# Moving the first norming of x and its transposes for the next chunk from half-steps 1 to 8 to half-steps 43 to 55 of the chunk in front

## The reference

```python
x = x + _L0_attn_ref(_layernorm(x, axis=-1), ...)   # q, k, v, rope, softmax(q k^T / 4) v, Wo
x = x + _L0_ffn_ref(_layernorm(x, axis=-1), ...)    # rms norm, top 2 of 8 experts, gated GELU-like unit
```

## Time and profile before

| | us |
|---|---|
| median of 3 runs | 1080.0 |
| lowest, highest | 1079.83, 1082.15 |
| profiled execution | 1079.36 |
| its span, first to last instruction | 1077.6 |
| PE busy | 945.4 |
| DVE busy | 759.1 |
| ACT busy | 749.9 |
| POOL busy | 402.8 |

### The profile page before, as it was taken

How to read it: one execution, slowest core, us unless ns; L and a number is a source line. 1 busy time by engine, 2 the same in 40 slices (tenths; PEclk the granted TensorE clock), 3 DMA queues, 4 the chain that set the end, 5 groups by cost and what they waited for, 6 DMA issues and landing times. The chain is left out here.

```text
span 1077.6 us, 16615 instructions
## 1 busy us (share of the span) xinstructions
PE 945.4 (88%) x5288; PEld 398.2 (37%) x5288; DVE 759.1 (70%) x1514; ACT 749.9 (70%) x1018; POOL 402.8 (37%) x341
## 2 busy tenths in 40 slices
PE   4669998899888997989899998889998999998396
PEld 2312213244332443334343443424442444344264
DVE  5851112689658885688858887588977786789797
ACT  1458895868668785877758786687878887885252
POOL 3515205343355324543353533653342333233310
PEclk9869999999899998999999998999999999999799
DMA  5273463424535452444533245354454453423021
GB/s 168 91 164 94 95 138 86 108 70 107 122 75 140 108 115 73 114 106 107 129 84 107 87 110 114 74 139 96 112 124 100 109 127 85 104 61 103 27 67 35
DMA packets 79984, 109.76 MB, mean 102 GB/s; under 512 B 22530, under 2 KB 56722, under 8 KB 76818
## 3 DMA queue, kind: packets, MB, share of 16 engines
q1 hardware_dynamic: 61460, 83.47, 33.2%
q10 hardware_dynamic: 18432, 25.17, 8.1%
HBM read 82.90 MB, written 25.69 MB: 101 GB/s over the span
## 5 line engine op out<-in xcount | busy, mean ns | idle before, releaser
L890 ACT ACTIVATE probs<-S 128x1024 f32<-128x1024 f32 x512 | 512.8, 1024 | 156.0 <-PE S L739 154.1
L739 PE MATMUL S<-Qs,Ks 98*128 98x512 bf16 x1024 | 301.4, 387 | 20.2 <-ACT probs L890 16.6
L753 PE MATMUL OP<-probs,V 128*17 128x512 f32 x2048 | 275.0, 609 | 3.6 <-ACT O L899 3.6
L977 POOL TENSOR_TENSOR act_lo<-act_sb,act_hi 128x512 fp32r<-128x512 f32 x112 | 150.2, 1344 | 112.9 <-ACT act_hi L879 112.8
L725 PE MATMUL D<-W,act_hi 128*128 128x256 f32 x448 | 132.9, 328 | 25.8 <-issue 14.4
L1196 DVE SCALAR_TENSOR_TENSOR acc<-D,combh,acc 128x256 f32<-128x256 f32 x224 | 97.6, 477 | 81.7 <-PE D L725 81.3
L739 PEld LDWEIGHTS S<-Qs,Ks 98*128 98x128 bf16 x1024 | 78.9, 99 | 204.0 <-ACT probs L890 97.8
L971 POOL TENSOR_SCALAR W<-W2b 128x512 fp32r<-128x512 bf16 x64 | 41.5, 650 | 238.3 <-PE D L725 193.2
L1204 DVE SCALAR_TENSOR_TENSOR th_sb<-th_sb,g_sb 128x512 f32<-128x512 f32 x112 | 109.2, 975 | 16.4 <-ACT th_sb L866 12.8
L725 PE MATMUL D<-W,act_lo 128*128 128x256 f32 x448 | 114.1, 286 | 0.0
L725 PEld LDWEIGHTS D<-W,act_hi 128*128 128x128 f32 x448 | 86.7, 194 | 51.2 <-issue 20.6
(11 more groups left out here) (173 smaller groups left out, 1007.2 us busy)
## 6 DMA issues: line engine op xcount, KB each, us to landing
W<-in_w ACTq DMA_DIRECT2D x64, 256.0 KB, 2.8
Ks<-k_scr SPq DMA_DIRECT2D x32, 384.0 KB
W2b<-in_w ACTq DMA_DIRECT2D x64, 128.0 KB, 2.8
Ks<-k_scr SPq DMA_DIRECT2D x32, 256.0 KB
o_scr<-O SPq DMA_DIRECT2D x32, 256.0 KB, 4.3
Qs<-q_scr SPq DMA_DIRECT2D x32, 192.0 KB
k_scr<-parts SPq DMA_DIRECT2D x12, 384.0 KB, 3.3
q_scr<-parts SPq DMA_DIRECT2D x12, 384.0 KB, 3.4
```

The lines of the kernel that those rows point to most:

```text
L739: last = mm(S[:, j2, C * i:C * (i + 1)], Ks[0:SROWS + MROWS, g % 2, j, P * kt:P * (kt + 1)], Qs[0:SROWS + MROWS, g % 2, j, :], start=True, ...
L753: last = mm(OP[32 * j:32 * j + VW, :], V[:, kt, HG * g + j, :], probs[:, s % 2, C * j:C * (j + 1)], start=kt == 0, stop=kt == KT - 1)
L890: nc.scalar.activation(probs[:, s % 2, 2 * C * j2:2 * C * (j2 + 1)], S[:, j2, :], ACT.Exp, scale=SCALE).then_inc(exp_done, 1)
L977: tt(act_lo[:, e % 2, it, :], act_sb[:, a % 2, :], act_hi[:, e % 2, it, :].bitcast(FP32), ALU.subtract).then_inc(lo_s, 1)
```

## The change

The four stages of the first norm and the two transposes leave PREP and form a table of their own, AHEAD. AHEAD in window u prepares chunk u + 3 (the one after the chunk whose queries and keys PREP makes in the same window), at half-steps 43 (`stats1`), 45 (`rstd1`), 49 (`xn`), 50 (`x_next`), 54 and 55 (`xT0`, `xT1`). In the next window the query/key tiles and values read `xnT` at the half-steps at which they read it before. Window 0 does both: the old places for chunk 2 (table PREP_FIRST) and AHEAD for chunk 3. So AHEAD runs in windows 0 to 4, and windows 1 to 5 have nothing of the norm in half-steps 1 to 8. In a half-step AHEAD comes after PREP and before POST and EXPERTS. The number of instructions of each kind in the kernel stays the same. The counters of the fillings are now counted in one pass, instead of restarted from computed constants, with the same meaning.

```diff
 
 
-    AT = {"x_next": 8, "stats1": 1, "rstd1": 1, "xn": 4, "xT0": 7, "xT1": 8, "qk0": 10, "qk1": 12, "qk2": 22,
+    AT = {"stats1": 43, "rstd1": 45, "xn": 49, "x_next": 50, "xT0": 54, "xT1": 55, "qk0": 10, "qk1": 12, "qk2": 22,
           "qk3": 30, "rope": 2, "part1": 3, "length": 5, "part2": 7, "part3": 10, "v0": 37, "v1": 42, "gmax": 1,
           "guard": 4, "flag": 6, "x1_in": 0, "wo_0": 8, "x1_b": 11, "wo0": 13, "wo1": 14, "stats2": 15, "rstd2": 16, "xc": 17, "ss":
           18, "ms": 18, "rrms": 20, "nf": 22, "nfT": 24, "logits": 26, "gates1": 26, "etop": 27, "gates2": 28,
           "combT": 32, "b20": 33, "b21": 34}
     FFN0, LAG, PAIRED = 26, 4, True
     DOWN, TANH, HIDDEN, UP, HI, LO, W2AT = 0, 2, 2, 1, 4, 6, 3
-    PREP = {}
+    PREP, PREP_FIRST, AHEAD = {}, {}, {}
     POST = {}
     EXPERTS = {}
 
     def place(table, half, *stages):
         table.setdefault(divmod(half, 2), []).extend(stages)
 
-    for st in ("x_next", "stats1", "rstd1", "xn"):
-        place(PREP, AT[st], (st, 0))
-    for a in range(2):
-        place(PREP, AT[f"xT{a}"], ("xT", a))
-        place(PREP, AT[f"v{a}"], ("v", a))
-    for a in range(4):
-        h = AT[f"qk{a}"]
-        place(PREP, h, ("qk", a))
-        for st in ("rope", "part1", "length", "part2", "part3"):
-            place(PREP, h + AT[st], (st, a))
-    for st in ("gmax", "guard", "flag"):
-        place(PREP, h + AT["length"] + AT[st], (st, 0))
-
+    FIRST = {"stats1": 1, "rstd1": 1, "xn": 4, "x_next": 8, "xT0": 7, "xT1": 8, "qk0": 10, "qk1": 12}
+    for table, at in ((AHEAD, AT), (PREP_FIRST, FIRST)):
+        for st in ("x_next", "stats1", "rstd1", "xn"):
+            place(table, at[st], (st, 0))
+        for a in range(2):
+            place(table, at[f"xT{a}"], ("xT", a))
+    for table, at in ((PREP, {}), (PREP_FIRST, FIRST)):
+        for a in range(4):
+            h = at.get(f"qk{a}", AT[f"qk{a}"])
+            place(table, h, ("qk", a))
+            for st in ("rope", "part1", "length", "part2", "part3"):
+                place(table, h + AT[st], (st, a))
+        for a in range(2):
+            place(table, AT[f"v{a}"], ("v", a))
+        for st in ("gmax", "guard", "flag"):
+            place(table, h + AT["length"] + AT[st], (st, 0))
     for st in ("x1_in", "wo_0", "x1_b", "stats2", "rstd2", "xc", "ss", "ms", "rrms", "nf", "nfT", "logits", "gates1", "etop",
                "gates2", "combT"):
         place(POST, AT[st], (st, 0))
...
             if late:
                 todo += [(st, a, before2) for st, a in EXPERTS.get((step + STEPS, place), [])]
             if prep:
-                todo += [(st, a, after) for st, a in PREP.get((step, place), [])]
+                todo += [(st, a, after) for st, a in (PREP if b or n else PREP_FIRST).get((step, place), [])]
+                ahead = (b + 1, n + 1) if n + 1 < NCH else (b + 2, 0)
+                if ahead[0] < B:
+                    todo += [(st, a, ahead) for st, a in AHEAD.get((step, place), [])]
             if post:
                 todo += [(st, a, before) for st, a in POST.get((step, place), [])]
                 todo += [(st, a, before) for st, a in EXPERTS.get((step, place), [])]
...
```

More of the change, by code:

```diff
@@ L136, in block_kernel, with __init__ @@
     FILLS = ("xT", "qk", "v", "length", "guard", "wo", "nfT", "logits", "combT", "b2")
-    PREP_FILLS = sum(st in FILLS and st != "guard" for l in PREP.values() for st, _ in l)
-    POST_FILLS = sum(st in FILLS for l in POST.values() for st, _ in l)
     class Beside:
[L143 to L151, removed]
+        def __init__(self):
+            self.n, self.last = 0, None
         def stages(self, b, n, step, place, prep, post, late):
@@ L385, in wait_apart @@
                 engine.sem_inc(passed, 1)
[L389 to L393, removed]
         def run(engine, beside, stage, attend, start, turn):
-            beside.at(0, 0, 0, False, False)
             for now in beside.head():
@@ L402, in run, with body @@
             turn(0)
-            def body(b, prep, base):
-                beside.at(base, b - 1, NCH - 1, True, looped(b) or b >= 1)
+            def body(b, prep):
                 for n in range(NCH):
@@ L414, in body @@
                     turn(b + 1)
[L416 to L421, removed]
+            for b in range(B):
+                body(b, b < B - 1)
             for step in range(FINAL + 1):
```

## The result

| | before | after |
|---|---|---|
| median, us | 1080.8 | 1064.2 (4 executions) |
| lowest, highest | 1079.83, 1082.15 | 1059.49, 1065.3 |
| profiled execution, its span | 1079.36, 1077.6 | 1064.35, 1062.5 |
| ratio to before, 95% interval | | 0.983, 0.981 to 0.985 |

Faster by 16.6 us by the medians and by 15.0 us between the profiled executions; the forecast was 19.35 us. In the kernel after, these lines stand 13 lower: L877 is the exponent (L890 before), L712 `down` (L725), L690 `up` (L703), L726 the scores (L739), L600 the query/key projection (L613), L651 the `b2` products that start the experts' sum (L664), L1105 their copies from `D` to `acc` (L1118).

The account below looks back on a forecast made before the run. PE's order was taken to set the pace, with the norm holding it up in windows 2 to 5. 28.65 + 0.6 - 9.9 = 19.35 us gained gave 1060.6 us; own range 1056 to 1066, wider range 1053 to 1073.

Parts of the forecast that it names:

- Early gain: Half-steps 0 to 12 of windows 2 to 5 become as in windows 6 and 7: 28.65 us gained.
- the third rival: Scaling chain or POOL's later work stops PE after half-step 12; only four waits go, 14.1 us: 1075 us; 8%.
- Window 1: `wo0` comes earlier without the `xnT` wait, until POOL's product limits it: 0.6 us gained, bounds 0 and 2.8.
- Statistics, power and `xn` at no cost: At half-steps 43, 45 and 49 these fit into idle of DVE and POOL: cost 0.
- Transposes: At half-steps 54 and 55: 1.5 us in windows 2 and 4, 2.3 in 1 and 3, 1.3 in window 0.
- The 0.5 for `x_next`: Load at half-step 50 delays the reads of the sums on SP: 0.5 us per odd window, bounds 0 and 1.9.
- I take nothing for it: After half-step 12, POOL's product and sum come later relative to PE, query/key tiles push `wo0` back: 0 us.
- The first: Full stretch hides little; DVE's and PE's added work lands on the path: gain 3.6 us, 1076 us; 12%.
- The second: PE stalls at the new place as at the old, clock included: 9.3 us slower, 1089 us; 8%.
- The fourth: DVE copies `xnT` without queueing, only PE's 0.9 us per window is paid, 4.9 in all: 1055.6 us; 12%.

Follow-up runs that it names:

- b_rstd3: Kernel before, with only the power `rstd1` on POOL moved from half-step 1 to 3: 1073.7 us, ratio 0.994.
- after_again: The changed kernel run and profiled once more, with nothing altered: 1065.7 us, ratio 0.987.
- b_b2act: Kernel before, with the copy of the first `b2` tile out of `D` done by ACT instead of DVE: 1088.0 us, ratio 1.006.
- a_xT_early: Changed kernel, with the transposes back at half-steps 7 and 8 of the window that uses them: 1064.7 us, ratio 0.984.
- p4: Changed kernel, with the rotary product `part1` one half-step later and the `acc` copy still on DVE: 1064.6 us, ratio 0.984.
- a_xnT_act: Changed kernel, with both `xnT` copies on ACT outside the head: 1063.3 us, ratio 0.984.
- a_b2act: Changed kernel, with the copy of the first `b2` tile out of `D` done by ACT instead of DVE: 1068.2 us, ratio 0.989.
- a_both: Changed kernel, with the first `b2` copy and both `xnT` copies on ACT: 1068.9 us, ratio 0.988.
- a_b21_36: Changed kernel, with the second `b2` tile at half-step 36 instead of 34: 1080.4 us, ratio 0.998.
- p4_b2act: Changed kernel, with the first `b2` copy on ACT and `part1` one half-step later: 1051.9 us, ratio 0.972.
- p4_both: Changed kernel, with the first `b2` copy and both `xnT` copies on ACT and `part1` one half-step later: 1050.4 us, ratio 0.970.

## Why the prediction was right, and where it missed

The parts that the prediction named came to 28.3 + 0.45 - 9.1 = 19.65 us, against 19.35 forecast. What it left out took 4.6 us of that away again.

**Early gain: right.** 28.65 forecast, 28.3 measured, and by the mechanism named: `b_rstd3` takes away the 3.5 us waits by moving the power alone. The 14.1 us that the third rival gives "if only the four waits go" were more than that case brought: `b_rstd3` gave 11.2, since `xn` then makes a wait of its own, of 1.9 to 2.4 us, with a low clock behind three of the four.

**Window 1: right, within its scatter.** 0.6 forecast, 0.45 measured; `after_again` in place of after would have given -0.1. The limit was POOL's product, as said, and PE's wait for it moved from L600 to L665.

**Statistics, power and `xn` at no cost: right, with less cover than it seems.** The power was over 2.3 us before the `w2`; `xn` was held by an `act_lo` and took 2.39 us instead of 1.38, and the `acc` behind it still freed `D` in time.

**Transposes: right in sum (9.1 against 9.9), one part empty.** Even windows: 1.5 forecast, 1.54 measured. Window 0: 1.3 forecast, 0.7 measured. Odd windows: 2.3 forecast, 2.7 measured. The 0.5 for `x_next` wasn't there. SP in window 3, the big load and then the sums:

```profile
498.44 0.40 SPq L467 DMA_DIRECT2D X<-in_x  x1
499.09 1.73 SPq L495 DMA_DIRECT2D sums_c<-o_scr  x4
```

The load stands right ahead of the sums, as forecast; but their last read lands 2.9 us after its issue (median of the view of transfers), near 503.7 at the latest, and DVE's reciprocal comes at 506.54, with no idle ahead of it.

**What the sum left out.** First, half-steps 12 to 16: "I take nothing for it" was a gain of 0.4 us in each of windows 2 to 5, 1.6 in all. It goes with the place of the transposes: these half-steps take 13.54 us in every trace with the transposes early (before, `b_rstd3`, `b_b2act`, and `a_xT_early`, where all else is late), and 13.14 to 13.16 in all with them late. Which wait it is wasn't looked for. Second, and larger, the clock at half-step 36, 7.6 us. The prediction read the wait of 3.5 us and the clock at the old place, and took every other stretch over unchanged. In the trace of before the wait of 1.65 us stood in each of windows 1 to 5, with a clock of 1.00 in four of them, so it was read as a fixed length. It is one only by chance: `after_again` and `p4` put the long stretches into other windows. Windows 0, 6 and 7, which don't have this wait, show the low clock at that place in no trace. Without that term the change would have given 22.6 us, or 1057 us. In part the profiled execution of before was a lucky one: its mean granted clock was 0.964, that of fifteen others lay between 0.956 and 0.964 with a mean of 0.960, and their median time was 1081.5. The fastest execution of after, 1059.5 us, had 0.970, its profiled one 0.961.

**The rivals.** The first (all of it on the path, 1076) was wrong: `xn` and the statistics cost nothing. The second (stall at the new place) didn't occur at half-steps 43 to 50. The third asked whether another wait takes the early gain; in windows 2 to 5 none did. The fourth (4.9 us for the transposes) was wrong too: in window 2 DVE stood idle for 0.50 us ahead of its `xnT` copy, so there was no queue, and 1.54 us were paid all the same. That clock is paid for elsewhere was in no rival.

```profile
383.03 0.69 DVE L1024 COPY xnT<-D 128x512 f32<-128x512 f32 x1 [0.50 <-PE D L594]
```

**Open.** Whether the change makes the low clock at half-step 36 likelier isn't settled. In the seven traces whose wait there is 1.65 us, the clock was low in 6 of 10 windows (1 to 5) of before and `b_rstd3`, and in 17 of 25 of after, `after_again`, `a_xT_early`, `a_xnT_act` and `p4`: no difference to speak of, with one to five windows of five from execution to execution. But the medians give the change 15.9 to 16.6 us and not 22.6, and the typical execution of before is only 2.1 us above its profiled one (1081.5 against 1079.4), so the one lucky trace doesn't account for all of the 7.6 us.

## What to carry to other kernels

A short instruction costs what stands behind it in its engine's queue. Moving the statistics, the power and `xn` to where POOL was idle was worth 24.5 us (101.25 to 76.7) for 4.3 us of work per window, while moving the transposes with them lost 2.7 us by the pieces. And two engines can be late for one cause: here a copy had to change its engine and a product its half-step before the wait went, and either alone brought nothing or a loss. Of a PE wait as long as the 1.65 us here, count the clock behind it as well, even if this profile shows it at full speed; a wait is worth its length at least, and here nearly three times that where the clock fell (1.65 us and 3.0). Compare stretches with equal instruction counts between two traces, the untouched ones too.

## What the runs showed of the hardware

The same wait of 1.65 us on PE was followed by a clock of 1.00 over half-steps 36 to 40 in some windows and of 0.68 to 0.81 (a mix of 1.2 and 2.4 GHz) in others, within one execution, and by a low one in 23 of 35 windows over seven traces; waits of 2.15 us and over there were followed by a low clock in 17 of 20 windows (`a_b2act`, `a_both`, `b_b2act`, `a_b21_36`), one of 1.02 us in none of ten (`p4_b2act`, `p4_both`). The Trainium skill, "TensorE: Matmul & The Clock Gate", "What's actually happening", says that the throttled clock is the default and activity lifts it; the direction agrees. What decides between the two kinds of windows no run here shows.

Some DVE work that ran into an instruction of POOL took longer by about what was left of that one: `xn` 2.39 and 2.62 us instead of 1.38 beside an `act_lo` of 1.3 us, `act_sb` 1.64 instead of 0.69 beside the last 1.1 us of the rotary sum. Other work did not, with half a microsecond or more of a POOL instruction left: in `after` 16 `l_sb`, which read the PSUM bank `BB`, took 0.74 us as they do alone, 41 `acc` additions out of `D` 0.48, and 11 reciprocals 0.24. The Trainium skill, "SBUF — State Buffer", "SBUF: two separate sides", calls this an exclusive lock of the shared port for a whole instruction, and names of VectorE's instructions only those in a two-port mode or with two inputs in SBUF. The sizes agree, and so does it that not all are held. Here it spread GpSimd's lateness to an engine that waited for nothing of GpSimd's.
